# Gathering in steps of 16 slots, writing the experts' loop out on TensorE and ScalarE, and turning the experts' outputs ahead of the segment sums

## The chip, the cores and the metric

The kernel runs on one core of one Trainium2 chip. The time is the device time of one execution in microseconds (us), the median of three runs. In the profile PE is TensorE (PEld its weight loads), DVE is VectorE, ACT is ScalarE, POOL is GpSimd and SP is SyncE, which issues plain DMAs.

## What is computed

Two blocks of a small vision model on an input of 4 images, 128 channels, 32 x 32 positions, so 4096 tokens ("nodes") of 128 features. The first block (a deformable convolution and a feed-forward layer on the better half of the tokens) and the second block's convolution are not touched. The change lies in the last layer: a graph attention over 524288 random edges that decides how four experts are mixed.

```python
h = (x_flat @ W_gat).reshape(M, HEADS, NUM_EXPERTS)         # 4 heads x 4 experts = 16 numbers per node
e = leaky_relu(a_src[src] + a_dst[dst], 0.2)                # one per edge and head
ee = exp(e - segment_max(e, dst)[dst])
alpha = ee / segment_sum(ee, dst)[dst]
agg = segment_sum(h[src] * alpha[:, :, None], dst) + b_gat
scores = layernorm(agg).reshape(M, HEADS, NUM_EXPERTS).mean(1)
w = softmax(top_2(scores))
for ei in range(NUM_EXPERTS):
    out += g[ei] * (gelu(x @ W1[ei] + b1[ei]) @ W2[ei] + b2[ei])    # x: 4096 x 128, hidden 256
```

The edge indices are clipped to the 4096 nodes by the gathers and the segment sums, so nearly all edges either drop out or end at the last node; the kernel finds the few thousand that matter before this layer begins.

## The kernel before, in words

Every engine has its own instruction stream, written out by hand; semaphores alone order them. Nothing is scheduled by a planner. The last layer starts about 804 us into the span and runs these strands side by side:

- **The gather (POOL, DVE).** The edges that matter lie in 128 partitions, each with up to 128 slots sorted by target node. `N_STEPS`, the number of steps of 8 slots that the fullest partition needs, is computed on DVE (L1242 to L1244: add `STEP - 1`, shift right by 3) and read into a register. In each step `gather` (L577) on POOL does two halves: it waits until DVE is done with that half's buffer (`max1_done`), copies 4 columns of indices to `g_idx` (L583), and issues 4 indirect DMAs (L588), each of which fetches one table row of 20 numbers for each of the 128 partitions. `slot_step` (L1355) on DVE does, for each half, three picks (L1363 a one-hot of the target's bucket, L1365 its product with the targets' terms, L1367 the sum) and then waits for the rows and takes them over (L1371, L1372). `max1_done` lets POOL run two halves ahead.
- **The experts (PE, ACT).** For each of the 8 chunks of 512 tokens and each of the 4 experts, PE multiplies into the hidden layer (`hidden`, two matmuls, PSUM banks 2 and 3) and ACT applies Gelu (L788); PE multiplies back (`expert_out`, two accumulated matmuls) and ACT copies the result to `y_exp` (L793). PE has chunk 0 written out and chunks 1 to 7 in a hardware loop (L1894); ACT has all 8 in a hardware loop (L795). In a hardware loop the count that a wait asks for, and the chunk's address, come from registers.
- **Segment sums.** When the last step is done, DVE runs `slot_scans` (L1379 on): max scan, differences, ACT's exponentials (L815, asked for with `e_ask`), the product L1392, five more scans (L1398). PE turns them (L1914), ACT copies them (L818), 128 small matmuls (L1552) sum them per node, DVE merges them (`slot_merge`, L1407 on) and computes the score, the top 2 and the gates (L1484 to L1518). This chain asks ACT for a square root (L833) and for an exponential (L836).
- **Turning the outputs.** `turn_outputs` (PE, L1897) transposes all 32 pieces of `y_exp` by four 128 x 128 transposes into banks 2 to 5, and `keep_turned` (ACT, L802) copies them back. PE calls it behind the segment sums (L1933); ACT does the copies of 4 chunks ahead of the square root and those of the other 4 ahead of the exponential.
- **Mixing.** With gates and turned outputs there, DVE and ACT build diagonal matrices (L1524, L842, L1531), PE multiplies, DVE adds to X (L1539), and SP stores.

All steps of the gather end before the scans; the scans need ACT; ACT comes to the scans' exponentials only when its experts are done.

## Time and profile before

| | |
|---|---|
| median of 3 runs | 1075.08 us (1070.51 to 1075.96) |
| profiled execution, its own time | 1066.97 us |
| its span, first to last instruction | 1065.2 us |
| busy: PE, DVE, ACT, POOL | 798.7, 666.0, 364.2, 173.5 us |
| mean granted TensorE clock | 0.882 of 2.4 GHz |

The profile is of one execution. Times count from the start of the span. A busy engine is one with an instruction in work; register, branch and semaphore instructions are not counted. "Idle before" names the time an engine stood still before an instruction, and what ended it: another engine's instruction, a DMA, "issue" (nothing the profile can show) or "remote" (a semaphore whose sender the profile cannot name). A granted clock of 1.00 is 2.4 GHz, 0.50 is 1.2 GHz.

### The profile page before, as it was taken

To read this page: it belongs to the slowest core of one execution; us is meant where nothing else is said; L and a number is where in the kernel's file an instruction comes from. 1 tells how busy PE (TensorE), PEld (TensorE's weight loads), DVE (VectorE), ACT (ScalarE), POOL (GpSimd) and SP (SyncE) were. 2 spreads that over 40 slices of the span, in tenths; PEclk is the share of its full clock that TensorE was granted. 3 is DMA by queue.
4 is the path that set the end of the run, shared out by engine and by line. 5 is a ranking of instruction groups with operands and counts; after the bars stand their busy time and mean duration, and the time that the engine had idled before them with its cause. 6 is when DMAs were issued, how large, how long until landed. Compare 5 with 4: busy or idle time off the path is not lost.

```text
span 1065.2 us, 14646 instructions
## 1 busy us (share of the span) xinstructions
PE 798.7 (75%) x4525; PEld 497.0 (47%) x4565; DVE 666.0 (63%) x1427; ACT 364.2 (34%) x559; POOL 173.5 (16%) x201
## 2 busy tenths in 40 slices
PE   4359920017998989989988788799859969766768
PEld 1212210016887868878853233344316324223757
DVE  3699778755656656647648776586564533334567
ACT  4421130004544544534452233340021625346350
POOL 5180010000000000000022000100001576760011
PEclk9589965557999999999999899999978989988689
DMA  8000000010000000000000000000010010110001
GB/s 311 0 1 1 1 0 0 2 43 39 2 1 0 0 0 0 0 0 0 0 0 1 0 0 0 2 1 0 2 42 14 6 7 7 7 7 0 3 1 79
DMA packets 11421, 15.50 MB, mean 15 GB/s; under 512 B 5568, under 2 KB 9152, under 8 KB 10992
## 3 DMA queue, kind: packets, MB, share of 16 engines
q1 hardware_dynamic: 8288, 13.87, 3.6%
q0 software_dynamic: 3088, 1.08, 1.5%
q8 instruction: 22, 0.36, 0.1%
q14 instruction: 23, 0.19, 0.1%
HBM read 10.35 MB, written 4.59 MB: 14 GB/s over the span
## 4 chain that ended last, share of the span: by engine, by line
PE 29%; DVE 13%; issue 6%; another core or an unknown queue 3%; ACT 3%; DVEq 1%; POOL 0%; ACTq 0%; DMA 0%; PEld 0%; PEldq 0%; POOLq 0%; SPq 0%
PE banks L1552 25%; DVE kept L1227 2%; PE banks L1904 2%; DVE wide_buf L1187 1%; PE banks L1833 1%; DVE wide_buf L1193 1%; DVE tie L1191 1%; DVE kept L1290 1%; DVE T L865 1%; DVE round_k L1289 1%; PE banks L1585 1%; ACT wide_buf L775 1%; ACT XP L788 0%; DVE shared L1398 0%
## 5 line engine op out<-in xcount | busy, mean ns | idle before, releaser
L1136 DVE TENSOR_TENSOR wide_buf<-banks,small 128x1024 f32<-128x1024 f32 x72 | 88.2, 1224 | 117.8 <-ACT small L725 117.8
L1552 PE MATMUL banks<-wide_buf 128*128 128x256 f32 (+1 forms) x720 | 144.5, 348 | 0.0
L1552 PEld LDWEIGHTS banks<-wide_buf 128*128 128x128 f32 x720 | 122.2, 194 | 12.5
L1552 PE MATMUL banks<-XP 128*128 128x32 bf16 (+1 forms) x1168 | 101.0, 227 | 35.8 <-DVE XP L990 27.4
L1552 PE MATMUL banks<-taps_w,small 128*128 128x128 f32 x618 | 92.3, 296 | 20.4 <-issue 20.4
L723 ACT ACTIVATE small<-banks,neg_x 128x512 f32<-128x512 f32 x72 | 49.5, 687 | 150.6 <-remote 64.7
L1552 PEld LDWEIGHTS banks<-taps_w,small 128*128 128x128 f32 x618 | 85.6, 203 | 31.1 <-issue 21.5
L1552 PEld LDWEIGHTS banks<-XP 128*128 128x128 bf16 (+1 forms) x1168 | 62.0, 109 | 75.0 <-issue 45.7
L588 POOL DMA_INDIRECT rows_g<-table_d,g_idx x88 | 84.9, 965 | 37.6 <-issue 32.9
L1552 PE MATMUL banks<-T,XP 128*128 (+1 forms) x128 | 69.1, 660 | 20.5 <-issue 10.6
L739 ACT COPY wide_buf<-banks 128x512 f32<-128x512 f32 (+1 forms) x87 | 49.6, 570 | 96.5 <-PE banks L1552 95.8
L1552 PE MATMUL banks<-shared,sel 128*128 x180 | 52.3, 386 | 35.5 <-DVEq L1129 26.8
L990 DVE TENSOR_TENSOR XP<-lo_b,XP 128x2048 bf16<-128x2048 bf16 x64 | 77.8, 1215 | 0.0
L1552 PE MATMUL banks<-XP,rows_g 128*32 128x512 f32 x144 | 63.9, 603 | 2.5 <-issue 2.5
L1552 PE MATMUL banks<-XP,taps_w 128*128 x144 | 62.1, 593 | 1.2 <-ACT wide_buf L775 1.2
L622 ACT ACTIVATE shared<-T 128x512 f32<-128x512 f32 x32 | 20.1, 629 | 116.9 <-DVE T L853 116.9
L1552 PE MATMUL banks<-X,mean_w 128*128 128x512 f32 x64 | 35.1, 670 | 30.4 <-DVE X L1322 15.9
L788 ACT ACTIVATE XP<-banks,m_b 128x512 f32<-128x512 f32 x64 | 43.4, 687 | 36.1 <-PE banks L1552 19.2
L1552 PEld LDWEIGHTS banks<-T,XP 128*128 128x128 f32 x128 | 24.8, 206 | 59.0 <-issue 37.0
L725 ACT ACTIVATE small<-small 128x512 f32<-128x512 f32 x72 | 45.4, 631 | 2.3
L1552 PEld LDWEIGHTS banks<-XP,taps_w 128*128 128x128 f32 x144 | 27.1, 189 | 35.6 <-issue 35.6
L547 POOL COPY small<-T 128x1024 f32 x3 | 3.1, 1039 | 248.6 <-PE banks L1552 248.6
(341 smaller groups left out, 1210.8 us busy)
## 6 DMA issues: line engine op xcount, KB each, us to landing
wide_buf<-in_edges SPq DMA_DIRECT2D x2, 1536.0 KB, 14.7
generic_d<-generic SPq DMA_DIRECT2D x1, 2064.0 KB, 7.3
X<-in_x SPq DMA_DIRECT2D x4, 512.0 KB, 4.9
out_x<-X SPq DMA_DIRECT2D x4, 512.0 KB, 2.6
rows_g<-table_d,g_idx POOLq DMA_INDIRECT x88
wide_buf<-in_edges SPq DMA_DIRECT2D x2, 512.0 KB, 9.4
XP<-in_m_w SPq DMA_DIRECT2D x2, 512.0 KB, 4.8
taps_w<-in_w_dcn SPq DMA_DIRECT2D x1, 576.0 KB, 16.7
```

What stands on the lines that cost most here:

```text
L588: pool.indirect_dma_start(rows_step[:, half, k, :], None, table_d, bass.IndirectOffsetOnAxis(ap=g_idx[:, c:c + 1], axis=0)).then_inc(rows_ ...
L622: nc.scalar.activation(squares[:, i % 6, :], T[:, i, :], ACT.Square).then_inc(ln.squared, 1)
L723: nc.scalar.activation(hat_x[:, h, :], ps[2][:, :], ACT.Abs, bias=neg_x[:, :]).then_inc(ax_done, 1)
L725: nc.scalar.activation(hat_x[:, h, :], hat_x[:, h, :], ACT.Relu, bias=1.0, scale=-1.0).then_inc(rx_done, 1)
L739: nc.scalar.copy(out, tiles.rearrange("p (t c) -> p t c", c=P)).then_inc(yt_done, 1)
L775: nc.scalar.activation(routed[:, q * CHUNK:(q + 1) * CHUNK], ps[4 + q % 2][:, :], ACT.Relu, bias=neg_lo[:, :]).then_inc(turned_out, 1)
L788: nc.scalar.activation(mid[:, e % 2, c, :], ps[2 + c][:, :], ACT.Gelu, bias=m_b1[:, e, c:c + 1]).then_inc(mid_done, 1)
L990: return nc.vector.tensor_tensor(out_, digits.rearrange("p (a b) -> p a b", b=2).unsqueeze(2).to_broadcast(grid), lane_pair[:, 0:out_.shap ...
L1136: nc.vector.tensor_tensor(near_w[s % RING], banks[:, 0:2, :], hat_x[:, h:h + 1, :].to_broadcast([P, 2, CHUNK]), ALU.mult).then_inc(w_done, 1)
L1227: last = nc.vector.max(kept2[:, 8 * c:8 * c + 8], parts[:, c, :])
L1552: return nc.tensor.matmul(o, l, r, start=start, stop=stop, **kw)
L1904: last = nc.tensor.transpose(ps[2 + e][:, j * P:(j + 1) * P], y_exp[e][:, i, j * P:(j + 1) * P], ident[:, :])
```

## The change

Three edits. First, a step is 16 slots in place of 8 (`STEP`), still in two halves, so POOL copies 8 indices and issues 8 indirect DMAs for each half, into twice the buffer, and the three picks of DVE are done once for a step, on 16 slots, ahead of both halves. Second, the experts' loops on PE and ACT are Python loops: every chunk has its own instructions, with constants where registers were. Third, PE calls `turn_outputs` right behind the experts, ahead of `slot_sums`, and ACT calls `keep_turned(0, CHUNKS)`, now written out too, right behind its experts, ahead of everything that the segment sums ask of it.

```diff
-STEP = 8
+STEP_BITS = 4
+STEP = 1 << STEP_BITS
...
-        rows_step = rows_g[:, 0, :, :].rearrange("p (a k) f -> p a k f", a=2)
+        rows_step = rows_g
...
-        oh_slots = shared[:, 3200:3200 + HALF_STEP * HIS].rearrange("p (k t) -> p k t", t=HIS)
-        pick_grid = shared[:, 0:HALF_STEP * HEADS * HIS].rearrange("p (k h t) -> p k h t", h=HEADS, t=HIS)
+        oh_slots = shared[:, 3200:3200 + STEP * HIS].rearrange("p (k t) -> p k t", t=HIS)
+        pick_grid = shared[:, 0:STEP * HEADS * HIS].rearrange("p (k h t) -> p k h t", h=HEADS, t=HIS)
...
-                                                bass.IndirectOffsetOnAxis(ap=g_idx[:, c:c + 1], axis=0)).then_inc(rows_landed[half][k // 2], 16)
+                                                bass.IndirectOffsetOnAxis(ap=g_idx[:, c:c + 1], axis=0)).then_inc(rows_landed[half][k // (HALF_STEP // 2)], 16)
...
-            with act.Fori(0, CHUNKS) as i:
+            for i in range(CHUNKS):
                 hidden(i, 0)
                 for e in range(1, EXPERTS):
                     hidden(i, e)
...
             def keep_turned(first, last):
-                with act.Fori(first, last) as i:
+                for i in range(first, last):
...
+            keep_turned(0, CHUNKS)
             rest = act.value_load(num[0:1, N_REST:N_REST + 1], min_val=0, max_val=MAX_ROUNDS // WAYS - 1)
...
-            keep_turned(0, 4)
             act.wait_ge(f_ask, 2)
             nc.scalar.activation(stat[:, 1, :], stat[:, 1, :], ACT.Sqrt, bias=eps[:, 1:2], scale=1.0 / HE).then_inc(f_exp, 1)
-            keep_turned(4, CHUNKS)
             act.wait_ge(f_ask, 3)
...
-                run(nc.vector.tensor_scalar(steps_, steps_, 3, None, ALU.logical_shift_right))
+                run(nc.vector.tensor_scalar(steps_, steps_, STEP_BITS, None, ALU.logical_shift_right))
...
-            SLOT_KEYS, SLOT_STEP = 11, 2 * (3 + 1)
+            SLOT_KEYS, SLOT_STEP = 11, 3 + 2
...
+                cols = bass.ds(r * STEP, STEP)
+                grid = [P, STEP, HEADS, HIS]
+                step(nc.vector.tensor_tensor(oh_slots, ...
+                step(nc.vector.tensor_tensor(pick_grid, ...
+                step(nc.vector.tensor_reduce(z_by_head[:, :, cols].rearrange("p h k -> p k h"), pick_grid, AX_X, ALU.add))
                 for half in range(2):
                     cols = bass.ds(r * STEP + half * HALF_STEP, HALF_STEP)
-                    grid = [P, HALF_STEP, HEADS, HIS]
-                    step(nc.vector.tensor_tensor(oh_slots, ...
-                    step(nc.vector.tensor_tensor(pick_grid, ...
-                    step(nc.vector.tensor_reduce(z_by_head[:, :, cols].rearrange("p h k -> p k h"), pick_grid, AX_X, ALU.add))
                     for landed in rows_landed[half]:
-                        dve.wait_ge(landed, g * (16 * 2) + 16 * 2)
+                        dve.wait_ge(landed, g * (8 * HALF_STEP) + 8 * HALF_STEP)
...
-            with pe.Fori(1, CHUNKS) as i:
+            for i in range(1, CHUNKS):
                 experts(i)
...
+            turn_outputs()
...
                 pe.nop()
-            turn_outputs()
```

ACT's stream in the middle of the experts, before. An ISA row sets up a wait against a register, a REGISTER_ALU row computes one.

```order
L788 ACT_TABLE_LOAD
L788 ACTIVATE XP<-banks,m_b 128x512 [waits mid_ready]
L787 REGISTER_ALU
L788 ACTIVATE XP<-banks,m_b 128x512 [waits mid_ready]
L785 REGISTER_ALU
L787 ISA [waits my_ready]
```

And the same place after (lines stand one lower):

```order
L789 ACT_TABLE_LOAD [waits rounds_known,wc_in,mid_ready]
L789 ACTIVATE XP<-banks,m_b 128x512 [waits my_ready]
L789 ACTIVATE XP<-banks,m_b 128x512 [waits mid_ready]
L789 ACTIVATE XP<-banks,m_b 128x512 [waits mid_ready,my_ready]
```

The register and ISA rows are gone, and the table load stands ahead of chunk 0 only, no longer at the head of each chunk.

ACT's stream between the experts and the mixing, before (L807 are the copies of turned outputs, L815 the scans' exponentials):

```order
L793 COPY wide_buf<-banks 128x512
L824 ACT_TABLE_LOAD
L824 ACTIVATE vals<-vals 128x256 [waits f_ask]
L815 ACTIVATE f_w<-f_w 128x512 [waits e_ask] x2
L818 COPY small<-banks 128x4x128 [waits sums_turned] x6
L821 ACTIVATE vals<-vals 128x256 [waits e_ask]
L807 COPY wide_buf<-banks 128x512
L833 ACT_TABLE_LOAD
L833 ACTIVATE stat<-stat,eps 128x32 [waits f_ask]
L807 COPY wide_buf<-banks 128x512
L836 ACT_TABLE_LOAD
L836 ACTIVATE gate<-gate 128x128 [waits f_ask]
```

And after:

```order
L808 COPY wide_buf<-banks 128x512 [waits my_ready] x32
L826 ACT_TABLE_LOAD
L826 ACTIVATE vals<-vals 128x256 [waits f_ask]
L817 ACTIVATE f_w<-f_w 128x512 [waits e_ask] x2
L820 COPY small<-banks 128x4x128 [waits sums_turned] x6
L823 ACTIVATE vals<-vals 128x256 [waits e_ask]
L834 ACT_TABLE_LOAD
L834 ACTIVATE stat<-stat,eps 128x32 [waits f_ask]
L836 ACT_TABLE_LOAD
L836 ACTIVATE gate<-gate 128x128 [waits f_ask]
```

All 32 copies of turned outputs now stand ahead of the first exponential, and behind the square root and ahead of the last exponential there is only a table load.

DVE's stream of one step, before (its first half; the second has the same rows):

```order
L1363 TENSOR_TENSOR shared<-sel,lane 128x128
L875 REGISTER_ALU
L1365 TENSOR_TENSOR shared<-shared,bucket_dst 128x512 [waits m1_chain]
L1367 ISA [waits m1_chain]
L1367 TENSOR_REDUCE kept<-shared 128x4x4
L1369 ISA [waits m1_chain]
L1371 REGISTER_ALU [waits rows1_in,rows1_b]
L1371 COPY taps_w<-rows_g 128x16x4
L1372 TENSOR_TENSOR kept<-kept,rows_g 128x4x4
```

And after, the whole step but for a few register rows:

```order
L1362 TENSOR_TENSOR shared<-sel,lane 128x512
L1364 TENSOR_TENSOR shared<-shared,bucket_dst 128x2048 [waits m1_chain]
L1366 ISA [waits m1_chain]
L1366 TENSOR_REDUCE kept<-shared 128x16x4
L1372 REGISTER_ALU [waits rows1_in,rows1_b]
L1372 COPY taps_w<-rows_g 128x16x8
L1373 TENSOR_TENSOR kept<-kept,rows_g 128x4x8
L1372 ISA [waits m1_chain,rows2_in,rows2_b]
L1372 COPY taps_w<-rows_g 128x16x8
```

The three picks are four times as wide and stand once in a step; the second half has only its takeover left.

## Rows read from the trace of the kernel before

**Rows 1.** The chain of waits that ended last, from 800 on: start, us, what.
```profile
815.39 16.97 PE banks L1552 x64
...
835.11 14.00 PE banks L1552 x32
849.12 1.05 issue
...
862.92 2.67 another core or an unknown queue
```

**Rows 2.** Groups of lines, 815 to 973: busy, mean ns | idle before, releasers.
```profile
L588 POOL DMA_INDIRECT rows_g<-table_d,g_idx x88 | 84.9, 965 | 37.6 <-issue 32.9 <-POOL g_idx L583 4.1 <-DVEq L1374 0.6
...
L793 ACT COPY wide_buf<-banks 128x512 f32 x32 | 18.6, 586 | 52.8 <-remote 24.8 <-PE banks L1552 24.7 <-issue 3.4
...
L788 ACT ACT_TABLE_LOAD x7 | 9.0, 1283 | 0.1
```

**Rows 3.** One stretch: length, busy PE, PEld, DVE, ACT, POOL; clock, DMA share, GB/s.
```profile
847.00:875.00 28.00, 19.30 (x37) 7.26 (x35) 9.56 (x24) 9.60 (x15) 19.58 (x25) 0.88 0.10 7
```

**Rows 4.** Timeline of ACT, 857 to 975: start, duration, [idle before].
```profile
858.38 0.69 ACT L788 ACTIVATE XP<-banks,m_b 128x512 f32<-128x512 f32 x1 [0.77 <-remote]
862.86 0.58 ACT L793 COPY wide_buf<-banks 128x512 f32 x1 [3.79 <-PE banks L1552]
...
888.41 0.69 ACT L788 ACTIVATE XP<-banks,m_b 128x512 f32<-128x512 f32 x1 [0.16 <-issue]
...
972.01 0.58 ACT L793 COPY wide_buf<-banks 128x512 f32 x1 [1.13 <-PE banks L1552]
...
974.32 1.13 ACT L815 ACTIVATE f_w<-f_w 128x512 f32<-128x512 f32 x2
```

**Rows 5.** Timeline of PE, 860 to 868.
```profile
860.08 1.88 PE L1552 MATMUL banks<-XP 128*128 128x512 f32 x4
867.88 3.78 PE L1552 MATMUL banks<-XP 128*128 128x512 f32 x4 [5.92 <-ACT XP L788]
```

**Rows 6.** Timeline of DVE, 835 to 977.
```profile
835.03 0.29 DVE L1363 TENSOR_TENSOR shared<-sel,lane 128x128 f32<-128x128 f32 x1 [1.61 <-issue]
...
877.42 0.29 DVE L1363 TENSOR_TENSOR shared<-sel,lane 128x128 f32<-128x128 f32 x1 [2.60 <-issue]
...
958.53 0.69 DVE L1382 SCALAR_TENSOR_TENSOR kept<-kept 128x512 f32<-128x512 f32 x1 [0.40 <-DVE kept L1372]
...
960.84 0.69 DVE L1385 TENSOR_TENSOR f_w<-kept,sq 128x512 f32<-128x512 f32 x1 [0.24 <-DVE sq L1383]
...
975.08 2.29 DVE L1392 TENSOR_TENSOR shared<-taps_w,f_w 128x2048 f32<-128x2048 f32 x1 [11.78 <-ACT f_w L815]
```

**Rows 7.** Timeline of POOL, 820 to 956.
```profile
820.03 0.19 POOL L583 COPY g_idx<-sel 128x4 int32 x1 [73.87 <-DMA table_d<-shared]
...
838.35 0.26 POOL L583 COPY g_idx<-sel 128x4 int32 x1 [6.60 <-DVEq L1374]
...
949.48 0.20 POOL L583 COPY g_idx<-sel 128x4 int32 x1
...
954.23 0.94 POOL L588 DMA_INDIRECT rows_g<-table_d,g_idx  x1 [0.30 <-issue]
```

**Rows 8.** DMA queues, 832 to 957: packets, MB, share of 16 engines; the instruction queue.
```profile
q14 instruction: 1, 0.01, 0.0%
```

**Rows 9.** Groups of lines, 997 to 1027.
```profile
L807 ACT COPY wide_buf<-banks 128x512 f32 x32 | 16.5, 633 | 4.0 <-PE banks L1904 4.0
```

**Rows 10.** Stretches of PE at L1904: length, busy PE, PEld; clock, DMA share, GB/s.
```profile
1003.00:1009.20 6.20, 5.46 (x26) 5.46 (x26) 0.50 0.02 4
1009.50:1014.00 4.50, 4.50 (x44) 4.44 (x43) 1.00 0.00 0
```

**Rows 11.** Timeline of DVE, 1015 to 1025.
```profile
1015.62 0.35 DVE L1499 RECIPROCAL stat<-stat 128x32 f32<-128x32 f32 x1 [2.85 <-ACT stat L833]
...
1024.97 0.29 DVE L1515 SCALAR_TENSOR_TENSOR gate<-cand,gate 128x128 f32<-128x128 f32 x1 [4.07 <-ACT gate L836]
```

More of the change, by code:

```diff
@@ L1358, in slot_step @@
                 step, n = chained(m1_chain, g * SLOT_STEP, True)
+                cols = bass.ds(r * STEP, STEP)
+                grid = [P, STEP, HEADS, HIS]
+                step(nc.vector.tensor_tensor(oh_slots, his[:, cols].unsqueeze(2).to_broadcast([P, STEP, HIS]),
+                                             lane[:, 0:HIS].unsqueeze(1).to_broadcast([P, STEP, HIS]), ALU.is_equal))
+                step(nc.vector.tensor_tensor(pick_grid, oh_slots.unsqueeze(2).to_broadcast(grid),
+                                             bucket_dst[:, :, :].unsqueeze(1).to_broadcast(grid), ALU.mult))
+                step(nc.vector.tensor_reduce(z_by_head[:, :, cols].rearrange("p h k -> p k h"), pick_grid, AX_X, ALU.add))
                 for half in range(2):
                     cols = bass.ds(r * STEP + half * HALF_STEP, HALF_STEP)
-                    grid = [P, HALF_STEP, HEADS, HIS]
-                    step(nc.vector.tensor_tensor(oh_slots, his[:, cols].unsqueeze(2).to_broadcast([P, HALF_STEP, HIS]),
-                                                 lane[:, 0:HIS].unsqueeze(1).to_broadcast([P, HALF_STEP, HIS]), ALU.is_equal))
-                    step(nc.vector.tensor_tensor(pick_grid, oh_slots.unsqueeze(2).to_broadcast(grid),
-                                                 bucket_dst[:, :, :].unsqueeze(1).to_broadcast(grid), ALU.mult))
-                    step(nc.vector.tensor_reduce(z_by_head[:, :, cols].rearrange("p h k -> p k h"), pick_grid, AX_X, ALU.add))
                     for landed in rows_landed[half]:
-                        dve.wait_ge(landed, g * (16 * 2) + 16 * 2)
+                        dve.wait_ge(landed, g * (8 * HALF_STEP) + 8 * HALF_STEP)
                         dve.sem_inc(passed, 1)
```

## Prediction

> **What bounds the kernel now.** Read first the chain of waits that ended last, over the stage that the change touches (it begins about 804 us into the span). It runs through PE's expert matmuls: chunk 0 and the start of chunk 1 as one piece to 832.4, then a chunk as 14.00 us of unbroken matmuls and a gap of 1.05 us before the next [rows 1]. Then the regularity stops: from 850 on the chain is broken by pieces put down to "another core or an unknown queue". Were all chunks like the one at 835.11, the last would end near 832.4 + 7 x 15.05 = 937.7; ACT's last expert copy ends at 972.01 + 0.58 = 972.6 [rows 4]. So some 35 us of the experts' 140 are lost. The reader should look for them in three views. By stretches: in 847 to 875, 28 us, PE is busy 19.3 and its clock still 0.88, so the clock alone is not it [rows 3]. By lines: ACT stood still 52.8 us ahead of its 32 copies, and half of that is "remote", no sender known [rows 2]. By time: ACT has a gap of 0.77 us between two Gelus where 0.16 is usual, and one of 3.79 us ahead of a copy whose input PE had long made; PE then waits 5.92 us for ACT [rows 4, 5]. The stalled engine is ACT, and PE follows.
>
> DVE shows the same in the same stretch (2.60 us ahead of L1363, by "issue") [rows 6]. What the stalls have in common is the kind of row between the instructions: wherever I find one, a register row or a wait against a register stands in between (one REGISTER_ALU between the two Gelus, a REGISTER_ALU and an ISA wait ahead of the copy, the loop's end ahead of L1363). PE's four passes at 860.08, with only constants between, take 1.88 us in the middle of it, as everywhere [rows 5]. What slows the register rows the trace doesn't say; it happens only while the gather runs.
>
> Beside it the gather ends almost as late: POOL's last indirect DMA ends at 955.17, DVE begins the scans at 958.53 [rows 6, 7]. DVE is ready for the product L1392 at 963.3 and gets ACT's exponential only at 975.08, 11.78 us later [rows 6]. So the gather has 11.8 us of slack, and behind it the experts decide. Behind that, two short waits for ACT: 2.85 us for the square root and 4.07 us for the exponential, both queued behind copies of turned outputs [rows 11].
>
> **Steps of 16.** 88 indirect DMAs are 11 steps of 8 [rows 2], so the fullest partition has 81 to 88 slots, and now takes 6 steps of 16: 96 DMAs, 8 more. POOL's cost: its halves start 5.85 us apart on average (838.35 to 949.48 is 19 halves, stalls of about 1.7 us among them, so 5.76 without) [rows 7]. Four more DMAs at 0.95 busy and 0.30 between (the last row of that group) are 5.0 us, so a half of 8 takes 10.76 us and 12 take 129.1. From the first copy at 820.03 that is 949.2. It would be dearer than 22 x 5.76 = 126.7, but for the start: before, POOL had two halves of 4 out and stood still for 6.60 us until DVE, which comes to its first pick at 835.03, gave a buffer back. Now its first two halves last until 841.6. DVE's picks on 16 slots: 0.69 for 512 elements, 2.3 each for two operations on 2048 (what L1392 takes for 2048), with gaps 5.9 us; it starts at 835.03, is done at 840.9, takes the first half over and returns it at about 841.8. POOL waits 0 to 1 us, I take 0.7. Later the picks stand in the 10.8 us of POOL's other half and cost nothing; if DVE stalls as at 877, they have 4 us to spare. With that and 0.6 of jitter the last DMA ends at about 950.5, the scans start 3.36 us later (958.53 - 955.17), at 953.9: 4.6 earlier. The extra 8 slots are empty everywhere, so all 128 partitions read the same row. No row shows that alone; between nothing and 3 us more for landing, I take nothing beside the 3.36, since the last halves of before already held mostly empty slots.
>
> **Experts written out.** Seven table loads of 1.28 us go [rows 2], and with them PE's seven gaps of 1.05 [rows 1]. All register rows go from ACT's and PE's expert code. Undisturbed, PE needs 832.4 + 7 x 14.00 = 930.4, and ACT's last copy ends near 931. Bounds: no stall left, 931; all of the 35 us left, 966. I take the first, since no instruction with constants alone is slow in the rows, and add nothing.
>
> The Trainium skill ("Runtime: NRT & Kernel Launch", Instruction fetch mechanics) says that a taken branch whose target is outside the two pages in the buffer forces a fetch. The trace does not show that cost in these loops: the instruction queues moved one packet in 832 to 957 [rows 8]. So the gain of writing out can't be saved fetches, and a straight stream brings fetches of its own; by the page's rule they run ahead and are hidden.
>
> **Turned outputs ahead of the sums.** The 32 copies take 16.5 us of ACT, 0.52 each [rows 9]; PE's 128 transposes take 44 in 4.50 us at full clock, 13.1 in all, and 26 in 5.46 at half clock, 26.9 in all [rows 10]. At full clock ACT sets the pace: 931 + 16.7 = 947.7. At half clock PE does: 958.0. PE comes out of the experts at full clock, and in [rows 10] it stays full over the transposes; I take 947.7. Then come the table load (1.28), the Exp of node_w (0.4), and ACT is free at 949.4. DVE asks for the first exponential when L1385 is done, 3.0 us behind the scans' start [rows 6], at 956.9. The cover is thus 7.5 us; each us of the experts beyond that goes to the end. What is queued behind the moved copies on ACT are exactly those exponentials, and behind PE's transposes those of the sums, for which DVE waits.
>
> The Trainium skill ("TensorE: Matmul & The Clock Gate", transpose section) says that transposes don't count as activity for the full clock. By that the turn would run at half clock and end at 958.0, ACT would be free 2.8 us behind DVE's asking, and the end 1.5 us later. The trace disagrees: here the clock rose to 1.00 with transposes alone in front of it [rows 10].
>
> So L1392 starts 4.8 us behind the scans' start plus the wait's 0.15: DVE was ready at 963.3, which is 4.77 behind 958.53. 953.9 + 4.95 = 958.9 in place of 975.08: **16.2 us** earlier. The chain from there to the scores is the same code. At the square root 2.75 of 2.85 us go. At the exponential 3.55 of 4.07 go, since its table is now loaded while DVE still computes: **6.3 us**. PE is idle longer ahead of the mixing, but its clock had already fallen there; the first chunks may be 2 us dearer or cheaper. DVE paces the mixing anyway.
>
> **Sum.** 16.2 + 6.3 = 22.5 us. The profiled execution took 1066.97 us (1065.2 of span and 1.8 around it), which gives 1044.5. But the runs' median is 1075.08, 8.1 above it. If the difference lies in the stalls, which look like chance, they go too and 1044.5 stands; if it lies elsewhere, it is 1052.6. I take 1048.
>
> **Rivals.**
> - *ACT stalls whatever its waits look like* (slower or no gain). What slows ACT is then not the register rows but the gather's traffic or its own semaphores. Experts end at 972.6 less PE's seven gaps, 965.2; the turn now stands ahead of the exponentials: 981.9 at full clock, 992.1 at half; + 1.28 + 0.42 + one exponential of 0.56 [rows 4], L1392 at 984.2 to 994.4, 9.1 to 19.3 later, less 6.3: 2.8 to 13.0 us slower, 1070 to 1080 by the profiled execution, 1078 to 1088 by the median. It decides from turned copies that end beyond 979, that is experts beyond 962. For it: DVE and ACT are slow together, so the cause is common. Against: PE's plain passes and POOL's steady 1.25 us. Point 1082.
> - *Half of the stalls stay.* Experts at 948.5, copies at 965.2, L1392 at 967.5: 7.6 + 6.3 = 13.9 gained, 1053 to 1061. Point 1057. Same mechanism, waits on constants slow too but less.
> - *The wider picks hold POOL back.* DVE stalls hit the picks and each step loses 3 to 4 us: 6 x 3.5 = 21 later scans, so L1392 at 980 and nearly nothing gained, 1066 to 1075. For it: 2.60 us stalls on DVE. Against: 4 us to spare in each step, and fewer register rows in it than before. Point 1070.
>
> **How the numbers follow.** A run of this kernel tells no change from one below 0.5%, 5.4 us. The forecast 0.74 (its own range 1041 to 1055), half the stalls 0.10, wider picks 0.05, ACT stalls 0.11. Low end: the forecast's 1044.5 less 4 for a clock that rises early, 1040. Left out at the top are the last two rivals, so the high end is that of the half stalls and a part of the third: 1066. Faster: 0.74 + 0.10 + a part of the third and none of the fourth, 0.86; same: 0.06; slower: 0.08, the worse part of the ACT rival.
>
> **What would show it.** Right: in the profile after 96 indirect DMAs at 1.25 us without the 6.60 us wait, the last ending near 950; one table load ahead of the experts; a chunk every 14.0 us in the chain, no "remote" ahead of ACT's copies, PE's last expert pass near 930; copies of turned outputs ending near 948 at clock 1.00; L1392 waiting for nothing; L1499 and L1515 idle under 0.6 us. Wrong: gaps of 0.77 and 3.8 us on ACT with constants in its waits, or L1392 waiting for ACT beyond 965.

## The result, and the profile after

The changed kernel takes 1099.81 us (median of 4 runs, 1085.99 to 1108.56), the kernel before 1072.8 beside it (1069.41 to 1075.96). The ratio, which leaves out the longest run, is 1.0209, with a 95% interval of [1.0106, 1.0313]: slower, by 22 us as the ratio has it, where 1048 us was predicted. The profiled execution is that longest one, 1108.56 us (span 1106.8); the one of the kernel before was the shortest of its runs (1066.97). So the two traces lie 41.6 us apart where the medians lie 27, and the trace below shows the change at its worst.

First the chain of waits (start, duration, what ran or was waited for). Before, a chunk was 14.00 us of matmuls [rows 1]. Now the chain is in pieces until 959, and whole again from there on:

```profile
890.98 5.68 another core or an unknown queue
...
914.38 6.41 another core or an unknown queue
...
926.43 6.37 another core or an unknown queue
...
940.61 6.38 issue
947.58 7.19 issue
...
959.77 43.12 PE banks L1553 x92
1004.25 15.02 ACT wide_buf L808 x32
...
1020.04 1.28 ACT L826
...
1022.41 2.30 DVE shared L1393
```

The line groups from 815 to 1004, the same experts as in [rows 2] (busy us, mean ns, then idle time ahead and what ended it):

```profile
L589 POOL DMA_INDIRECT rows_g<-table_d,g_idx x96 | 98.0, 1021 | 35.2 <-issue 32.7 <-POOL g_idx L584 2.5
...
L789 ACT ACTIVATE XP<-banks,m_b 128x512 f32<-128x512 f32 x64 | 43.7, 687 | 51.1 <-PE banks L1553 24.1 <-remote 22.0 <-issue 3.1
...
L794 ACT COPY wide_buf<-banks 128x512 f32<-128x512 f32 x32 | 18.8, 586 | 71.1 <-remote 30.9 <-PE banks L1553 25.6 <-issue 14.6
```

ACT stood still 71.1 us ahead of its 32 expert copies, where it was 52.8 [rows 2]. Each copy is as short as ever. On the timeline the gaps are not the 0.8 and 3.8 us of before but 6 and 7, each time ahead of a single instruction. ACT's rows at the end of the gather and behind the experts, and in a fence of their own PE's:

```profile
932.82 0.59 ACT L794 COPY wide_buf<-banks 128x512 f32<-128x512 f32 x1 [6.39 <-remote]
935.72 0.69 ACT L789 ACTIVATE XP<-banks,m_b 128x512 f32<-128x512 f32 x1 [2.31 <-remote]
939.92 0.69 ACT L789 ACTIVATE XP<-banks,m_b 128x512 f32<-128x512 f32 x1 [3.52 <-remote]
946.99 0.59 ACT L794 COPY wide_buf<-banks 128x512 f32<-128x512 f32 x1 [6.38 <-issue]
954.77 0.59 ACT L794 COPY wide_buf<-banks 128x512 f32<-128x512 f32 x1 [7.19 <-issue]
...
1002.91 0.59 ACT L794 COPY wide_buf<-banks 128x512 f32<-128x512 f32 x1 [1.13 <-PE banks L1553]
1004.25 15.77 ACT L808 COPY wide_buf<-banks 128x512 f32<-128x512 f32 x32 [0.75 <-PE banks L1905]
```

```profile
928.19 1.88 PE L1553 MATMUL banks<-XP 128*128 128x512 f32 x4
940.66 3.78 PE L1553 MATMUL banks<-XP 128*128 128x512 f32 x4 [10.59 <-issue]
944.24 2.31 PE L1553 MATMUL banks<-T,XP 128*128 128x512 f32 x4
959.77 3.78 PE L1553 MATMUL banks<-T,XP 128*128 128x512 f32 x4 [13.23 <-ACT XP L789]
...
1003.55 15.22 PE L1905 MATMUL banks<-ident,wide_buf 128*128 128x128 f32 x128 [0.68 <-ACT wide_buf L794]
```

PE still runs its four passes in 1.88 us (3.78 right behind a long wait), and then stands still 10.6 and 13.2 us. The experts' code holds constants only here. In 925 to 960, the end of the gather, PE is busy 11.18 of 35 us; from 960, when no transfer runs any more (DMA share 0.00), 42.88 of 43 (the stretches' columns as in [rows 3]):

```profile
925.00:960.00 35.00, 11.18 (x17) 3.87 (x16) 6.90 (x11) 4.79 (x8) 23.59 (x26) 0.70 0.17 8
960.00:1003.00 43.00, 42.88 (x92) 18.04 (x92) 3.99 (x5) 22.07 (x35) 0.00 (x0) 0.94 0.00 0
1003.00:1020.00 17.00, 15.85 (x132) 14.04 (x132) 0.00 (x0) 16.25 (x33) 0.00 (x0) 1.00 0.00 0
```

The gather itself on POOL, runs of 8 DMAs behind one copy of indices, and what DVE does beside the long one at 838.82:

```profile
831.47 0.20 POOL L584 COPY g_idx<-sel 128x8 int32 x1
832.46 0.97 POOL L589 DMA_INDIRECT rows_g<-table_d,g_idx  x1 [0.79 <-issue]
...
838.82 1.94 POOL L589 DMA_INDIRECT rows_g<-table_d,g_idx  x1 [0.30 <-issue]
841.06 0.94 POOL L589 DMA_INDIRECT rows_g<-table_d,g_idx  x1 [0.30 <-issue]
...
843.80 0.19 POOL L584 COPY g_idx<-sel 128x8 int32 x1 [0.54 <-issue]
...
955.64 0.94 POOL L589 DMA_INDIRECT rows_g<-table_d,g_idx  x1 [0.30 <-issue]
```

```profile
837.65 2.29 DVE L1364 TENSOR_TENSOR shared<-shared,bucket_dst 128x2048 f32<-128x2048 f32 x1
840.18 2.29 DVE L1366 TENSOR_REDUCE kept<-shared 128x2048 f32 x1 [0.24 <-issue]
...
960.00 0.69 DVE L1383 SCALAR_TENSOR_TENSOR kept<-kept 128x512 f32<-128x512 f32 x1 [0.40 <-DVE kept L1373]
...
964.08 0.69 DVE L1389 TENSOR_TENSOR f_w<-f_w,sq 128x512 f32<-128x512 f32 x1
1022.41 2.29 DVE L1393 TENSOR_TENSOR shared<-taps_w,f_w 128x2048 f32<-128x2048 f32 x1 [57.65 <-ACT f_w L817]
...
1066.46 0.29 DVE L1516 SCALAR_TENSOR_TENSOR gate<-cand,gate 128x128 f32<-128x128 f32 x1 [0.43 <-ACT gate L836]
```

The product starts at 1022.41 in place of 975.08 [rows 6], 47.3 us later. From it to the end of the span it is 1106.8 - 1022.41 = 84.4, where it was 1065.2 - 975.08 = 90.1: 5.7 given back. 47.3 - 5.7 = 41.6 is the whole difference of the two spans. The packing itself gained nothing: the last DMA ends at 955.64 + 0.94 = 956.58, where it was 955.17, and the scans start at 960.00, where it was 958.53.

### The profile page after: what moved, and what is told of

Read it like the earlier page. It is cut to its first block, busy times and chain, and to the rows that moved or that the text cites. A ratio compares the mean times of both kernels' runs of the same rounds, so it can differ in the third digit from the quotient of the medians.

```text
span 1106.8 us, 14005 instructions
## 1 busy us (share of the span) xinstructions
PE 804.8 (73%) x4525; PEld 496.5 (45%) x4565; DVE 653.5 (59%) x1359; ACT 355.0 (32%) x552; POOL 183.9 (17%) x199
## 3 DMA queue, kind: packets, MB, share of 16 engines
q0 software_dynamic: 3344, 1.16, 1.6%
## 4 chain that ended last, share of the span: by engine, by line
PE 26%; DVE 14%; issue 7%; ACT 5%; another core or an unknown queue 4%; DVEq 1%; POOL 0%; DMA 0%; PEldq 0%; PEld 0%; ACTq 0%; POOLq 0%; SPq 0%
PE banks L1553 24%; DVE kept L1227 2%; DVE wide_buf L1187 1%; ACT wide_buf L808 1%; ACT XP L789 1%; DVE wide_buf L1193 1%; PE banks L1834 1%; DVE tie L1191 1%; DVE kept L1290 1%; DVE T L865 1%; DVE round_k L1289 1%; PE banks L1586 1%; ACT wide_buf L776 1%; ACT wide_buf L794 1%
## 5 line engine op out<-in xcount | busy, mean ns | idle before, releaser
L589 POOL DMA_INDIRECT rows_g<-table_d,g_idx x96 | 98.0, 1021 | 35.2 <-issue 32.7
L1553 PE MATMUL banks<-T,XP 128*128 128x512 f32 x128 | 72.2, 683 | 40.7 <-ACT XP L789 38.3
L1553 PE MATMUL banks<-XP,rows_g 128*32 128x512 f32 x144 | 67.0, 627 | 2.5 <-issue 2.5
L1372 DVE COPY taps_w<-rows_g 128x128 f32 x12 | 3.8, 313 | 81.0 <-DMA rows_g<-table_d,g_idx 80.5
## 6 DMA issues: line engine op xcount, KB each, us to landing
wide_buf<-in_edges SPq DMA_DIRECT2D x2, 512.0 KB, 10.1
```

Of the source, the lines that this page charges most:

```text
L589: pool.indirect_dma_start(rows_step[:, half, k, :], None, table_d, bass.IndirectOffsetOnAxis(ap=g_idx[:, c:c + 1], axis=0)).then_inc(rows_ ...
L1553: return nc.tensor.matmul(o, l, r, start=start, stop=stop, **kw)
```

## Experiments

Each runs beside the kernel before on its own chip: its median there was 1062.6 (first four), 1068.9, 1070.9, 1068.2 and 1055.6 (last two), so only ratios and traces are compared between groups. Two readings serve for all: ACT's idle time ahead of its 32 expert copies (32.6 to 33.7 us where the experts are written out and nothing of them stalls), and the start of the last copy. Each is read from one execution, and executions of one kernel differ. The paragraph behind each expectation says which of its theories held.

**The three parts alone.** Only the experts written out:

```diff
-            with act.Fori(0, CHUNKS) as i:
+            for i in range(CHUNKS):
...
-            with pe.Fori(1, CHUNKS) as i:
+            for i in range(1, CHUNKS):
```

> Only the experts' loops on PE and ACT are written out; steps of 8 and the place of the turned outputs are as before. Theory U (written-out experts are stalled more by the gather than looped ones): the experts end on ACT near 1000 us into the span and the time is near 1095. Theory G (the stalls come with the gather and grow only because its halves are longer and POOL never pauses): the experts end near 965, seven table loads earlier than before, and the time is 1063 to 1068. Theory of the prediction (no stall without register rows): 931 and 1060, already refuted by the changed kernel's trace.

1055.64 us, ratio 0.9916 [0.9883, 0.9948]: faster, by less than 1%, and better than both theories. The group of ACT's copies, and DVE's product:

```profile
L793 ACT COPY wide_buf<-banks 128x512 f32<-128x512 f32 x32 | 18.8, 586 | 37.1 <-PE banks L1552 19.5 <-remote 11.2 <-issue 6.3
```

```profile
965.68 2.29 DVE L1392 TENSOR_TENSOR shared<-taps_w,f_w 128x2048 f32<-128x2048 f32 x1 [0.35 <-DVE f_w L1388]
```

The last copy starts at 943.4, the product waits for nothing of ACT's: the gather is the bound. Only the steps of 16 (the hunks with STEP, the picks and `rows_landed`):

> Only the gather is in steps of 16; experts looped, outputs turned behind the sums. Theory U: experts stall as before, 35 us, the time is within 4 us of before. Theory G: the experts end near 1000 and the time is 25 us above before.

1089.25, ratio 1.0233 [1.0146, 1.0321]: slower, as theory G had it. ACT's idle time is 63.4, its last copy at 994.5, the product at 997.55 behind a wait of 31.65. Only the turn moved (`turn_outputs()` and `keep_turned(0, CHUNKS)` behind the experts):

> Only the turned outputs are moved ahead of the segment sums; experts looped, steps of 8. Both theories: stalls of the experts as before, experts end near 973; the turn (16 us at full clock) stands ahead of the exponentials, so L1392's product starts near 991 in place of 975, and 6.3 us come back at the square root and the exponential: some 10 us slower than before.

1077.48, ratio 1.0136 [1.0100, 1.0173], slower as expected: ACT's idle time is 50.7, the last copy at 966.9, the product at 986.50 behind 24.45 of waiting, the turned copies among what it waits for. Steps of 16 and the turn, experts still in loops:

> The changed kernel with the experts' loops put back: steps of 16, outputs turned ahead of the sums. Theory U: stalls as in the kernel before, experts end near 973, 10 us slower than before, near 1083. Theory G: as the changed kernel plus the table loads, near 1105.

1097.98, ratio 1.0321 [1.0243, 1.0399], last copy at 993.3: theory G again. Thus the greater part of the loss comes with the steps of 16 (2.3% alone) and a part with the turn (1.4% alone). Writing out is a gain alone; on top of the two no gain clear of the noise is seen (1.0209 against 1.0321, not measured beside each other, with intervals that overlap).

**What of the gather does it.** On the changed kernel, every index its partition's own row, none shared:

```diff
-                step(nc.vector.tensor_tensor(slot_idx[:, 0:P], slot_idx[:, 0:P], slot_lo, ALU.add))
+                step(nc.vector.tensor_scalar(slot_idx[:, 0:P], neg_lo[:, 0:1].to_broadcast([P, P]), -32.0 / (1 << 17), None, ALU.mult))
```

> The changed kernel, but every slot's index is replaced by a row of its partition's own (row 32 x p in some order), so all 128 rows of each indirect DMA differ, empty slots among them; the attention's values are no longer the reference's. Theory H (an empty slot's index is row 4095 in every partition, and the many reads of one row are what stalls the experts): no stalls, ACT's last expert copy near 935 and the time near 1045. Theory P (the wide picks on DVE stall them) and theory Q (the run of indirect DMAs as such): as the changed kernel, last copy near 1003, time near 1097.

1085.91 (two runs), ratio 1.0191 [1.0068, 1.0315], ACT's idle time 64.2, last copy at 986.4: it stalls with no shared row. All indices the same row:

```diff
+                step(nc.vector.memset(slot_idx[:, 0:P], LAST))
```

> The changed kernel, but every slot fetches row 4095; values not the reference's. Theory H: the stalls of 890 to 955 are there from the first gather on, the last expert copy beyond 1015, the time beyond 1110. Theories P and Q: as the changed kernel, 1003 and 1097.

1062.69, ratio 0.9978 [0.9935, 1.0020], which no theory had: the opposite of what a shared row would do. POOL's queue took 2.4% of the DMA engines' span instead of 1.6 for the same 3344 packets, ACT's idle time is 36.7 and the last copy at 943.7:

```profile
L794 ACT COPY wide_buf<-banks 128x512 f32<-128x512 f32 x32 | 18.7, 585 | 36.7 <-PE banks L1553 18.3 <-issue 11.6 <-remote 6.7
```

POOL issues the same 96 DMAs here as in the changed kernel (100.9 us of busy time, 98.0 there), so POOL's own instructions alone don't set the stalls. Now no indirect DMAs at all, POOL only counts up the semaphores (DVE clears the buffer beforehand, so the segment sums work on zeros):

```diff
-                        pool.indirect_dma_start(rows_step[:, half, k, :], None, table_d,
-                                                bass.IndirectOffsetOnAxis(ap=g_idx[:, c:c + 1], axis=0)).then_inc(rows_landed[half][k // (HALF_STEP // 2)], 16)
+                        pool.sem_inc(rows_landed[half][k // (HALF_STEP // 2)], 16)
```

> The changed kernel with the 96 indirect DMAs left out (POOL raises their semaphores itself, the rows are zero); the values are not the reference's. Theories H and Q: no stall, chunks of 14.0 us, last expert copy 931 to 935, turned outputs end near 951. Theory P: the experts stall as long as the wide picks run, some 60 us now since they no longer wait for rows.

1039.9 (two runs), ratio 0.9760 [0.9659, 0.9860]. Nothing "remote" is left, each chunk is 14.0 us and the last copy starts at 932.8, though DVE's wide picks all run beside the experts:

```profile
L793 ACT COPY wide_buf<-banks 128x512 f32<-128x512 f32 x32 | 18.7, 585 | 33.7 <-PE banks L1553 33.7
```

DVE's picks in pieces of 4 slots, so that no DVE operation is 2.3 us long:

> The changed kernel, but the three picks of a step are done in 4 pieces of 4 slots, as wide as in the kernel before (512 elements), still ahead of both halves; everything is computed. Theory P: POOL's indirect DMAs of 1.9 to 2.1 us go, and the experts' stalls fall to those of the steps of 8: last expert copy near 945, time near 1055. Theories H and Q: stalls as in the changed kernel, within 0.5% of its time.

1107.66, ratio 1.0389 [1.0308, 1.0471], idle time 63.1, last copy at 1004.9. POOL's long DMAs are gone (96 in 92.3 us), the stalls are not: the width of the picks isn't it.

**The rhythm of the DMAs.** The changed kernel, with POOL's indices copied 4 at a time:

```diff
-                    nc.gpsimd.tensor_copy(g_idx[:, cols], ...)
...
-                    pool.wait_ge(idx1_ready, g * 2 + half + 1)
...
                     for k in range(HALF_STEP):
...
+                        if k % 4 == 0:
+                            nc.gpsimd.tensor_copy(g_idx[:, c:c + 4], slot_idx[:, bass.ds(r * STEP + c, 4)]).then_inc(idx1_ready, 1)
+                            pool.wait_ge(idx1_ready, g * 4 + half * 2 + k // 4 + 1)
```

> The changed kernel, except that POOL copies its indices 4 at a time with the wait behind each copy, as the kernel before does; halves stay 8 slots, takeovers, picks and buffers as changed. POOL's rhythm is then 4 DMAs, a break of about 1.0 us, 4 DMAs. Theory R (what stalls the experts is the length of an unbroken run of indirect DMAs, 8 instead of 4, and the rate of 1.37 us a DMA instead of 1.46): the experts' last copy falls back to about 944, as in the unrolled kernel with steps of 8, gather ends near 956, L1393 near 966, time about 1050 to 1056. Rival S (it is what the step of 16 is elsewhere: DVE's takeovers of 8 rows, 16 DMAs' buffers, landing counts of 4 DMAs each): the experts' last copy stays at 995 to 1005 and the time 1090 to 1105.

1062.20, ratio 0.9931 [0.9899, 0.9963], against 1.0209 for the changed kernel: theory R, with fewer stalls and a longer gather than it gave. ACT's copies of experts and of turned outputs, POOL, and DVE's product:

```profile
L794 ACT COPY wide_buf<-banks 128x512 f32<-128x512 f32 x32 | 18.7, 585 | 32.6 <-PE banks L1553 22.1 <-issue 10.5
...
L808 ACT COPY wide_buf<-banks 128x512 f32<-128x512 f32 x32 | 17.9, 590 | 12.6 <-PE banks L1905 9.4 <-remote 2.7 <-issue 0.3
```

```profile
870.66 0.94 POOL L589 DMA_INDIRECT rows_g<-table_d,g_idx  x1 [0.31 <-issue]
871.62 0.19 POOL L586 COPY g_idx<-sel 128x4 int32 x1
872.61 0.96 POOL L589 DMA_INDIRECT rows_g<-table_d,g_idx  x1 [0.80 <-issue]
```

```profile
977.27 2.29 DVE L1393 TENSOR_TENSOR shared<-taps_w,f_w 128x2048 f32<-128x2048 f32 x1 [0.35 <-DVE f_w L1389]
```

One pause of 0.7 us in the middle of each run of 8 (872.61 - 870.66 = 1.95 from start to start, where 1.25 is usual) takes every "remote" out of the experts' stage: idle 32.6, the last copy at 934.5 instead of 1002.9. Twelve such pauses cost the gather 8 us, and it is the bound now. But the stalls are not all gone. The turn behind the experts still runs beside this gather, and there ACT stands still 12.6 us ahead of its copies, where it was 0.7 in the changed kernel: from the experts' end to its own it takes 965.5 - 935.1 = 30.4 us, not 16.5. It has cover, so the time doesn't show it. Indices 2 at a time:

> The same with indices copied 2 at a time: a break of about 1.0 us after every second DMA, 1.6 us a DMA over 96, so the gather ends near 974 by POOL alone. Theory R: hardly a stall, the experts' last copy at 935 to 944, but the scans at 978 and L1393 at 983, time about 1060. Rival S: the experts' last copy at 995 or later, as the gather that stalls them also lasts longer, time 1095 to 1110.

1079.12, ratio 1.0085 [1.0059, 1.0111], where 1060 was expected: idle 33.7, last copy at 932.7, product at 992.90, set by the gather. The turn too runs unbroken here, 16.5 us with 0.7 of idle time, beside DMAs all the while. Steps of 8, experts written out and the turn moved, so the change without its steps of 16:

> Steps of 8 as before, experts written out, turned outputs behind the experts: the change without its steps of 16. Theory: stalls as in the unrolled kernel with steps of 8, the experts' last copy near 944, turned copies to 961, table and Exp to 962.7; the scans start at 960.6, DVE asks at 965.5 and L1392 starts at 965.7 unwaited. The waits for square root and exponential go (2.85 and 4.07 before): about 6 us below that kernel, near 0.986 of the kernel before. Rival: the experts' stalls come as in the looped kernel with the turn moved (last copy 967 there): turned copies to 984, L1392 at 987, and the ratio is 1.005 to 1.01.

1072.92 over 1061.95 to 1082.16, ratio 0.9980 [0.9936, 1.0024], between the theory and its rival. In the profiled run the idle time is 42.3, the last copy at 957.8 and the product at 977.70 behind 10.92 of waiting. The rhythm of 4 still stalls somewhat here, and differently from run to run. Halves of 2 slots, experts written out, the turn where it was:

> Experts written out, turn where it was, and steps of 4 slots, halves of 2: the other side of the change's scale (2, 4, 8 slots a half). POOL copies indices and waits for its buffer after every 2 DMAs. Theory R and rival S agree in direction: fewer stalls than with halves of 4, the experts' last copy at 932 to 940. POOL's half takes 2 x 1.25 + 0.73 = 3.2 us plus DVE's answer, with at most 4 DMAs ahead: the gather ends at 965 to 985, and the time is set by it, 1060 to 1080. If neither holds and the stalls are tied to how long the gather runs, the experts end at 960 or later.

1073.42, ratio 1.0042 [1.0009, 1.0074]; idle 33.7, last copy at 933.1, product at 983.50, the gather again. Now a break without a wait, one more copy that nothing reads:

```diff
...
+                        if k == 4:
+                            nc.gpsimd.tensor_copy(idle_idx[:, 4 * half:4 * half + 4], slot_idx[:, bass.ds(r * STEP + c, 4)]).then_inc(idx1_ready, 1)
```

> The changed kernel, with one more POOL copy of 4 indices (into a place that nothing reads, and not waited for) in the middle of each run of 8 DMAs: a break of 0.2 to 0.3 us more instead of the 0.98 with a waited copy. Theory R1 (any break that cuts the runs to 4 is enough): the experts' last copy near 935 as with waited copies, gather 6 us shorter than there, L1393 near 970, time 1054 to 1058. Theory R2 (the break must be long enough for what is queued to drain, the rate decides): stalls stay for the most part, the experts' last copy beyond 965, time 1075 to 1100.

1083.79 over 1064.10 to 1089.93 in 4 runs, too scattered for a ratio. The traced run is the longest, its last copy at 985.6. POOL, and ACT's copies:

```profile
910.88 0.94 POOL L592 DMA_INDIRECT rows_g<-table_d,g_idx  x1 [0.30 <-issue]
911.83 0.19 POOL L591 COPY idle_idx<-sel 128x4 int32 x1
912.18 0.97 POOL L592 DMA_INDIRECT rows_g<-table_d,g_idx  x1 [0.16 <-issue]
```

```profile
L797 ACT COPY wide_buf<-banks 128x512 f32<-128x512 f32 x32 | 18.7, 586 | 59.8 <-remote 32.3 <-PE banks L1556 19.2 <-issue 8.3
```

The expectation had the break wrong: from start to start it is 1.30 us, only 0.05 more than usual, since the copy stands in the gap that is there anyway. So it tests hardly a break at all, and the stalls stay (59.8). It shows that an instruction between the DMAs doesn't end them; the run with 0.7 us between does so for the experts. One of the four runs took 1064.10, so here too they come in some executions more than in others. Experts in loops again, on the changed kernel with indices 4 at a time:

> Steps of 16 with indices copied 4 at a time, but the experts in loops again on ACT and PE: are the register rows part of it? If the gather's rhythm alone decides: no stall, chunks of 15.05 us (14.00 and the table loads' gap), the experts' last copy near 942, turned copies to 959, L1393 set by the gather at 977, time 1060 to 1064. If register rows stall by themselves in a gather of such a rhythm: gaps as before, the experts' last copy at 965 or later, time 1072 to 1085.

1063.27, ratio 0.9965 [0.9934, 0.9996]; idle 35.8, no "remote", last copy at 941.5. This settles what my forecast rested on: with all their register rows back, the experts don't stall. The turn behind them does, 12.0 us of idle time and 29.7 us in all. Next, on the same kernel with experts written out, the last half of 8 left out where it is empty everywhere (a number N_ODD beside N_STEPS, and on POOL and DVE):

```diff
+            with pool.If(odd > 0):
...
+                gather(last, last, 1)
...
+            with dve.If(odd > 0):
...
+                slot_step(0, last, 1)
```

> Steps of 16 with indices copied 4 at a time, and the last half of 8 left out where no partition has slots in it (88 DMAs instead of 96; POOL and DVE branch on one number). Theory: no stalls, so the gather is the bound, and each DMA less counts. 22 pieces of 4 at 5.70 us and five waits of some 1.2 us end near 955 instead of 968, scans at 958, L1393 at 963 instead of 977.3; turned copies end at 950.4, ACT is free at 952. Time near 1048, about 14 below the kernel with 96. Rival: what ended the stalls there was a chance of phase, and they come back here: experts' last copy beyond 950, L1393 beyond 970, time 1055 to 1080.

1053.42 (1051.19 to 1056.48), ratio 0.9877 [0.9829, 0.9926]: faster than both kernels, though 5 us slower than expected. The experts don't stall (33.0, last copy at 938.7); this execution begins the gather 3.6 us later than that of the kernel with 96 DMAs, and the turn takes 29.8 us from the experts' end instead of 16.5, so the product still waits:

```profile
971.42 2.29 DVE L1402 TENSOR_TENSOR shared<-taps_w,f_w 128x2048 f32<-128x2048 f32 x1 [3.09 <-ACT f_w L822]
```

```profile
950.00:960.00 10.00, 6.37 (x26) 4.65 (x27) 3.28 (x5) 3.70 (x7) 7.32 (x9) 0.52 0.15 7
```

In this stretch, turn beside gather, PE's clock is 0.52. With 96 DMAs and indices 4 at a time, takeovers of 4 on DVE, as with steps of 8:

> Steps of 16 with indices copied 4 at a time and 96 DMAs, and DVE takes the rows over 4 at a time, as the kernel with steps of 8 does: its takeover is the one thing in which that kernel's gather, equal in rhythm, still differs inside a step. If the takeovers of 4 (with their register rows on DVE while the next rows arrive) cause the stalls that the unrolled kernel with steps of 8 shows: gaps on ACT again, the experts' last copy at 942 to 960, time 1062 to 1075. If not: no stall, the last copy at 934.8, time 1060 to 1064, and what is left is the number of DMAs ahead of DVE (16 here, 8 there).

1064.08, ratio 0.9975 [0.9937, 1.0013], idle 32.6: not the takeovers. In the turn ACT stands still 14.4 us. The last two ran on a chip where the kernel before takes 1055.6. The kernel with steps of 8 and experts written out, its buffers put further apart:

```diff
-        rows_step = rows_g[:, 0, :, :].rearrange("p (a k) f -> p a k f", a=2)
+        rows_step = rows_g[:, :, 0:HALF_STEP, :]
```

> The kernel with experts written out and steps of 8, with its two halves of 4 rows in SBUF at the places where the kernels with steps of 16 have theirs (320 bytes further apart in each partition); nothing else. If the place of the buffers is why that kernel still stalls a little with a rhythm of 4: ACT's idle time ahead of its 32 expert copies falls from 37.1 to 33, the experts' last copy from 943.4 to 935; the time stays near 1055, as the gather is the bound. If not: 36 to 43 us and 943 to 958 as in the two kernels that have shown it.

1054.35, ratio 0.9992 [0.9977, 1.0008], idle 33.7. Picks and takeovers both in pieces of 4, with indices 4 at a time:

> Steps of 16 with indices copied 4 at a time, and on DVE both the takeovers and the picks in pieces of 4 slots, as with steps of 8: what then still differs from steps of 8 is how far POOL may run ahead of DVE (16 slots, not 8). If DVE's many small instructions with their register rows cause what stalls are left with a rhythm of 4: ACT's idle time ahead of the 32 copies rises from 32.6 to 40 or more, the experts' last copy beyond 942, time 1066 to 1085. If the distance ahead does, or chance: 33 us and 935, time 1062 to 1070 (the gather is the bound, and the picks in pieces take DVE some 1 us more a step).

1057.55, ratio 1.0018 [1.0001, 1.0034], idle 33.7. Neither stalls, and in the second the turn runs unbroken too, 16.5 us beside DMAs (idle 0.7). But on this chip the kernel before, whose experts are in loops, is itself 15 us faster than on another; no trace of it was taken here. So neither the place of the buffers nor the small pieces can be credited with it: inconclusive.

## Why the prediction was wrong

- *Experts written out, no stall left, 931.* This is the step that failed. Each stall that I saw had a register row in it, and I made the rows the cause. They were only where the stall was seen, and the row I held against them, PE's passes of 1.88 us, was no test: after the change they are as short between the longest stalls (928.19). Two runs show it: the loops' rows back beside an unbroken experts' stage, idle 35.8, and constants alone beside runs of 8 DMAs, idle 71.1. The cause is the gather's DMAs: without them nothing stalls, and with a pause of 0.7 us after every 4 the experts don't. The last copy ended at 1002.9 + 0.6 = 1003.5, 72.5 us beyond the forecast, and the cover of 7.5 us was gone nearly ten times over. The other three runs, 9 to 23 us shorter, presumably lost less.
- *Steps of 16.* I priced them by POOL's and DVE's own time. Of that held: 96 DMAs, no wait of 6.60 us any more, scans 3.4 us behind the last DMA. But it ended at 956.6, not at 950.5: seven of the DMAs took 1.5 to 2.1 us, beside DVE's operations on 2048 elements, 98.0 - 96 x 0.95 = 6.8 us in all. I had priced the wide picks as costing nothing. So the scans came 1.5 us later and not 4.6 earlier. What I also left out is what a denser run of DMAs does to engines that have no part in it.
- *The rival with the cause in common* named the mechanism ("the gather's traffic") and had 0.11. Its price, 1082, kept the stalls at 35 us; in the trace they grew to 70. It counted the gather's traffic as given, while the change itself makes it denser. "DVE and ACT are slow together" should have weighed more than the kind of row.
- *Turned outputs.* 32 copies in 0.75 + 15.77 = 16.5 us at clock 1.00, where 16.7 was forecast. Right for a turn with no gather beside it, which is not where I had put it: beside the gather, runs with unbroken experts took 29.7 to 32.0 us in four traces and 16.5 in two. The Trainium skill ("TensorE: Matmul & The Clock Gate", transpose section) says that transposes don't count as activity for the full clock; the trace disagrees here as it did before, since the stretch 1003 to 1020, transposes nearly alone, has 1.00. With the experts late, each of them stands ahead of the exponentials: the turn alone costs 1.4%. Moved work that stands behind late work is on the path.
- *Square root and exponential*: 6.3 us forecast; L1516 waits 0.43, L1500 not at all, so 6.5 of the 6.92 went, and from the product to the end 5.7 were gained.
- *One table load* ahead of the experts, seven gone: right. With nothing stalling the experts they are worth 1.0 us each: the last copy at 941.5 with the loops and at 934.5 without.

The sum failed in one great term and a small one. 22.5 us of gain needed experts at 931; with them at 1003.5, the same chain gives 1003.5 + 16.5 + 2.4 = 1022.4, the measured start of the product (2.4 is the table load, the Exp of node_w and one exponential, with gaps). And even with experts at 931 the scans at 960.0 would have put the product at 960.0 + 4.95 = 965.0, 10.1 us earlier than before and not 16.2.

**What stays open.** Kernels with steps of 8 have the same rhythm of 4, and still stalled in every trace but that on the last chip (37 to 53 us of idle time where 33 is free of stalls), with times that scatter by up to 20 us. With steps of 16 the rhythm of 4 freed the experts but not the turn. So the rhythm matters, and is not all of it. It needs no loops (37.1 with the experts written out), and takeovers of 4 don't bring it about. In that rhythm, small picks and the place of the buffers were tried only on the chip where the kernel before is fastest, so they stay open, with the chip, and with how far POOL may run ahead of DVE, 8 slots or 16, which wasn't tried. Nor do the runs say through what the DMAs reach ACT and PE: the rows show PE's passes at their usual length and the instruction that waits for them released microseconds late, which points at what lies between an engine's signal and its waiter, and not at the work itself. That is argued, not shown. That all indices on one row stall less (36.7), with the same DMAs at nearly the same pace but more time in the queue's packets, says that the pace of POOL alone doesn't decide; why it helps is open too.

## What to carry to other kernels

When several engines stall together while one kind of transfer runs, suspect the transfer, and leave it out in one run before you build on the rows around the stall. A change that packs small DMAs closer is not priced by its queue's own time: here the packing saved the gather nothing (its end at 956.6 for 955.2), and compute that neither waits for these DMAs nor reads what they bring ended 31 us later. Where a pause frees one stage, look at the next one too: here the stalls went on in the turn. And work that is moved ahead of a request needs its cover counted against the worst end of what stands before it.

## What the runs showed of the hardware

- Runs of 8 indirect DMAs, 1.25 us apart, made the matmul stage beside them up to 70 us longer (last copy at 1002.9 in the longest run, against 932.8 without DMAs). A pause of 0.7 us after 4 of them freed that stage (934.5), but not the transposes behind it; a POOL copy without such a pause did not free it (985.6, in its longest run).
- The same gather with all indices on one row kept POOL's queue busy longer (2.4% of the span against 1.6, 3344 packets each) and disturbed ACT less (idle 36.7 against 71.1).
- An indirect DMA of 0.95 us on POOL takes 1.5 to 2.1 when it meets DVE's f32 operations on 2048 elements (838.82 above; up to 3.1 in other runs). With picks of 512 elements the mean is 0.96 (96 in 92.3 us).
- 128 transposes ran at clock 1.00 in 15.22 us behind the matmuls with no gather. Beside one they took 28.7 us with the clock down to 0.52 in one run (88 DMAs, indices 4 at a time), and 15.21 at 1.00 in two others (indices 2 at a time; indices, picks and takeovers all 4 at a time).
